# One block for the sum, the norm, the router, the dispatch, the shared expert and q/k/v in a two-layer recurrent and mixture-of-experts kernel

## What is computed

```
xn = layernorm(x)                         # no weights
s  = mamba_like_mixer(xn)                 # layer 0: 64 heads, conv, chunked scan
f  = hadamard_ffn(xn)                     # layer 0: 256 -> 1024 -> 256
x  = x + s * silu(f)
xn = layernorm(x)
s  = causal_attention(xn)                 # layer 1: 16 heads of 16, q/k/v with biases
f  = shared(xn) * sigmoid(xn @ v) + sum of top-4 of 16 experts(xn)   # 704 / 176 hidden
x  = x + s * silu(f)
```

## Time and profile before

| | us |
|---|---|
| profiled execution, its own time | 2469.58 |
| its span | 2467.9 |
| TensorE busy (matmul) | 2181.8, 88% |
| VectorE busy | 1859.4, 75% |
| ScalarE busy | 1146.9, 46% |
| GpSimd busy | 1203.4, 49% |
| granted clock, mean | 0.945 |
| last instruction of the mixer on VectorE | ends 1613.5 |
| shared expert's first gate/up matmul | 1681.8 |
| expert weights asked for, 5632 and 2816 KB | 1790.0, 1790.3 |
| last of the q/k/v weights lands | 1828.2 |
| last value tile of `qkv` | ends 1885.5 |

### The profile page before, as it was taken

The page is one execution under the profiler, slowest core; times in us unless marked ns, Lnnn a source line. Parts: engine busy times, 40 slices in busy tenths (PEclk is TensorE's granted clock), DMA queues, the critical chain, the costliest instruction groups (busy, mean ns, idle before and its releaser), DMA issues. The chain is left out here.

```text
span 2467.9 us, 38890 instructions
## 1 busy us (share of the span) xinstructions
PE 2181.8 (88%) x12914; PEld 1682.4 (68%) x12914; DVE 1859.4 (75%) x3309; ACT 1146.9 (46%) x2397; POOL 1203.4 (49%) x1299
## 2 busy tenths in 40 slices
PE   4995899999999999999999999939946998899982
PEld 2784688888888888888888888728835776344432
DVE  4875788888888888888888888755734444888745
ACT  1331455555555555555555555413323333366660
POOL 3544366565665665656656654603402332999000
PEclk9997799999999999999999999968978999799996
DMA  2002000000000000000000000040053554343214
GB/s 92 1 14 78 30 3 3 33 3 33 3 3 33 3 3 33 3 14 22 3 33 3 3 3 3 3 170 12 1 185 121 179 176 145 107 121 119 78 63 159
DMA packets 76917, 128.87 MB, mean 52 GB/s; under 512 B 22747, under 2 KB 54587, under 8 KB 74715
## 3 DMA queue, kind: packets, MB, share of 16 engines
q1 hardware_dynamic: 69859, 107.64, 13.0%
q0 software_dynamic: 6864, 18.75, 3.1%
HBM read 91.81 MB, written 46.92 MB: 56 GB/s over the span
## 5 line engine op out<-in xcount | busy, mean ns | idle before, releaser
L1026 DVE SCALAR_TENSOR_TENSOR mix_cv<-mix_pp,mix_cw,mix_cv 128x384 f32<-128x384 f32 (+4 forms) x864 | 492.7, 570 | 25.1 <-ACT mix_cv L949 4.2
L873 PEld LDWEIGHTS mix_pyd<-mix_xdt,mix_lm 128*128 128x128 f32 x2048 | 247.8, 192 | 56.7 <-issue 53.1
L949 ACT ACTIVATE mix_cv<-mix_pp,mix_cb,mix_cw 128x384 f32<-128x384 f32 (+1 forms) x288 | 182.1, 632 | 211.2 <-PE mix_pp L80 211.2
L78 PE MATMUL mix_pp<-l0in_XH,mix_wx_lo 128*128 128x384 f32 (+2 forms) x576 | 238.3, 414 | 38.6 <-DVE mix_ss L1015 23.0
L812 POOL TENSOR_TENSOR mix_xdt<-mix_xtok,l_dt 128x512 f32<-128x512 f32 x128 | 133.5, 1043 | 277.9 <-ACT mix_xtok L976 277.9
L805 POOL TENSOR_TENSOR mix_t<-mix_t,mix_xd 128x512 f32<-128x512 f32 x112 | 144.4, 1289 | 219.3 <-DVE mix_t L1040 153.5
L924 PE MATMUL mix_pgt<-mix_wo,mix_gt 128*128 128x256 f32 x1024 | 244.9, 382 | 2.9 <-issue 2.2
L873 PE MATMUL mix_pyd<-mix_xdt,mix_lm 128*128 128x64 f32 x2048 | 243.2, 272 | 2.5 <-DVE mix_lm L1076 2.5
L1839 DVE TENSOR_REDUCE att_tops<-att_psc 128x1 f32<-128x512 f32 (+3 forms) x384 | 189.6, 549 | 48.3 <-PE att_psc L1787 31.5
L955 ACT ACTIVATE mix_pp<-mix_cv 128x384 f32<-128x384 f32 (+1 forms) x288 | 133.0, 462 | 161.6 <-DVE mix_cv L1026 158.8
L924 PEld LDWEIGHTS mix_pgt<-mix_wo,mix_gt 128*128 128x128 f32 x1024 | 184.2, 190 | 31.2 <-issue 9.2
(11 more groups left out here) (365 smaller groups left out, 5794.2 us busy)
## 6 DMA issues: line engine op xcount, KB each, us to landing
mix_w_raw<-in_w_in SPq DMA_DIRECT2D x8, 1280.0 KB, 5.8
y_d<-exp_ys SPq DMA_DIRECT2D x79, 128.0 KB, 1.7
a_part<-att_sums SPq DMA_DIRECT2D x32, 256.0 KB, 5.1
mix_ll<-cs SPq DMA_DIRECT2D x384, 4.0 KB
q<-q SPq DMA_DIRECT2D x12, 512.0 KB, 4.5
k<-k SPq DMA_DIRECT2D x12, 512.0 KB, 4.6
att_qs<-q SPq DMA_DIRECT2D x32, 192.0 KB
att_ks<-k SPq DMA_DIRECT2D x32, 192.0 KB
```

Source lines behind the costliest of these rows:

```text
L78: pe.matmul(out, l_lo, r_hi, start=start, stop=False)
L873: last = pe.matmul(pyd[:, h * HP:(h + 1) * HP], lm[p % 2][:, h, :], xdt[p % 2][:, h * HP:(h + 1) * HP], start=True, stop=True)
L949: act.activation(conv_tile(k), pp[k % 2][:, halo:cols], ACT.Identity, bias=cb[:, it // 2, ct:ct + 1], scale=cw[:, it // 2, ct, 3:4]).then_ ...
L1026: last = dve.scalar_tensor_tensor(out, of, cw[:, g, ct, 3 - d:4 - d], out, ALU.mult, ALU.add)
```

## The change

`combine`, `layernorm`, `shared_and_dispatch` and `qkv` become one block, `middle`. Its parts:

- The silu of layer 0's feed-forward result is taken at the end of `prelude` (tanh on ScalarE, one product on VectorE per block of 512 tokens) before the store.
- Sum, statistics and norm run per block of 512 tokens. Block 0's come first, those of blocks 1 to 3 stand behind units 0 to 5 on VectorE; their power is on GpSimd and their norm on ScalarE (`Identity` with scale and bias) at units 2, 4, 6. Transposes stand in front of units 3 to 8, logits in front of units 0, 5, 7, 9. The weight splits of units 2 to 5 stand behind the low parts of units 0 to 3 on GpSimd.
- The dispatch has 62 steps from unit 9 on, the prefix matmuls are at unit 15, the index matmuls before the third q unit. `opos` and `same` are made with one operation per index (128 operations) from a bfloat16 table; the 16 scaled copies are on ScalarE after units 22 and 23.
- The high and low parts of the units' hidden tile have two buffers instead of three.
- q/k/v weights are loaded at the start and split in units 19 to 21. A q/k unit has its first part and the second on ScalarE, one difference on VectorE, the third part on GpSimd, and one store from a ring of three buffers. Value tiles stand between the q/k units from the fifth on. The factor `DH ** -0.25` on q and k moves into the attention's exponential.
- Gate/up expert weights are asked for after the last sum, down weights on ScalarE's queue at q unit 4.

```diff
+                def gate(b):
+                    rows = X[:, b * 4:(b + 1) * 4, :]
+                    dve.wait_ge(ft_done, b + 1)
+                    dve.scalar_tensor_tensor(rows, ftanh[b], 1.0, rows, ALU.add, ALU.mult).then_inc(f_gated, 1)
...
+                act.wait_ge(cut3, 3)
+                act.wait_ge(turned, 6)
+                for b in range(NB):
+                    act.wait_ge(added, NU - NB + b + 1)
+                    act.activation(ftanh[b], X[:, b * 4:(b + 1) * 4, :], ACT.Tanh, scale=0.5).then_inc(ft_done, 1)
...
+        TURN_AT = {3: 2, 4: 3, 5: 4, 6: 5, 7: 6, 8: 7}
+        NORM_AT = {2: 1, 4: 2, 6: 3}
+        LOGIT_AT = {0: 0, 5: 1, 7: 2, 9: 3}
+        DONE_AT = (0,) * 9 + (3, 9, 15, 21, 27, 32, 39, 42, 48, 50, 52, 54, 56, 57, 60, 60, 60) + (62,) * 14
+        PREFIX_AT, IDX_AT = 15, 2
+        V_AT = 4
...
+                    if b == NB - 1:
+                        sp.dma_start(W[:, 0:WG_COLS], wg_d).then_inc(w_ld, 16)
...
+                    sp.wait_ge(p2_done, u + 1)
+                    sp.dma_start(dst[:, c * P:(c + 1) * P, t * TB:(t + 1) * TB].rearrange("k p t -> p k t"),
+                                 part[u % NR3]).then_inc(stored[u % NR3], 16)
...
+                def power(b):
+                    pool.wait_ge(step, 7 * (b + 1))
+                    pool.tensor_tensor(rstd[:, rows_of(b)], var[:, rows_of(b)], half[:, rows_of(b)], ALU.pow).then_inc(powered, 1)
+                    if b:
+                        pool.wait_ge(powered, 2 * b)
+                        pool.tensor_tensor(shift[:, rows_of(b)], neg[:, rows_of(b)], rstd[:, rows_of(b)], ALU.mult).then_inc(powered, 1)
...
+                power(0)
+                low(0)
+                low(1)
...
+                    if n in (1, 3, 5):
+                        power(n // 2 + 1)
+                    if n < NS - 2:
+                        low(n + 2)
...
+                    pool.wait_ge(p1_done, u + 1)
+                    pool.tensor_tensor(part[u % NR3][:, 2, :], h[u % 2][:, :], part[u % NR3][:, 1, :], ALU.subtract).then_inc(p2_done, 1)
...
+                def turn(p):
+                    pe.wait_ge(xn_ready, p + 1)
+                    wait(pe, lo_done, p if p > 1 else 0)
+                    for j in range(2):
+                        for k in range(KD):
+                            last = pe.transpose(bank_of(p)[:, k * 256 + j * P:k * 256 + (j + 1) * P],
+                                                XN[:, 2 * p + j, k * P:(k + 1) * P], ident[:, :])
+                    last.then_inc(transposed, 1)
...
+                    if n in TURN_AT:
+                        turn(TURN_AT[n])
+                    if n in LOGIT_AT:
+                        logits(LOGIT_AT[n])
...
+                    if u == IDX_AT:
+                        pe.wait_ge(dv, 57)
+                        pe.wait_ge(val_done, 2)
...
+                    if u < 4:
+                        pe.wait_ge(h_done, NU)
+                    else:
+                        pe.wait_ge(sub1, u - 3)
...
+                    if n in NORM_AT:
+                        b = NORM_AT[n]
+                        act.wait_ge(powered, 2 * b + 1)
+                        for t in range(b * 4, b * 4 + 4):
+                            last = act.activation(XN[:, t, :], X[:, t, :], ACT.Identity, bias=shift[:, t:t + 1], scale=rstd[:, t:t + 1])
+                            if t % 2:
+                                last.then_inc(xn_ready, 1)
...
+                    if n in (22, 23):
+                        act.wait_ge(dv, 56)
+                        for t in range((n - 22) * 8, (n - 21) * 8):
+                            last = act.activation(val[:, 4 * t:4 * t + 4, 0, :], same[:, 4 * t:4 * t + 4, :], ACT.Copy, scale=float(t))
+                        last.then_inc(val_done, 1)
...
+                for u in range(len(QK) + 1):
+                    if u < len(QK):
+                        act.wait_ge(mm, u + 1)
+                        wait(act, stored[u % NR3], 16 * (u // NR3))
+                        col = u // 8 * 2 + u // 4 % 2
+                        act.activation(part[u % NR3][:, 0, :], pz[u % 4][:, :], ACT.Identity, bias=bq[:, col:col + 1]).then_inc(p0_done, 1)
+                    if u >= 1:
+                        act.wait_ge(sub1, u)
+                        act.activation(part[(u - 1) % NR3][:, 1, :], h[(u - 1) % 2][:, :], ACT.Copy).then_inc(p1_done, 1)
+                    if u == IDX_AT + 2:
+                        act.wait_ge(split, NS)
+                        act.wait_ge(dv, 62)
+                        act.dma_start(W[0:EI // 2, WG_COLS:], wd_d).then_inc(w_ld, 16)
...
+                        dve.wait_ge(rows_out, 16 * NB)
+                        for i in range((j - 48) * 16, (j - 47) * 16):
+                            last = dve.tensor_scalar(opos[:, i, :], iota[:, :], posf[:, i:i + 1], None, ALU.is_equal)
                     elif j < 56:
-                        at = slice((j - 52) * 16, (j - 51) * 16)
-                        last = dve.tensor_tensor(same[:, at, :], tilef[:, at].unsqueeze(2).to_broadcast([P, 16, TILE_COLS]),
-                                                 table(C_IOTA, TILE_COLS).unsqueeze(1).to_broadcast([P, 16, TILE_COLS]), ALU.is_equal)
+                        for i in range((j - 52) * 16, (j - 51) * 16):
+                            last = dve.tensor_scalar(same[:, i, :], iota[:, 0:TILE_COLS], tilef[:, i:i + 1], None, ALU.is_equal)
...
+                def extra(n):
+                    if n + 1 in TURN_AT:
+                        tokens_lo(TURN_AT[n + 1])
+                    if n in (0, 2, 4):
+                        gate(n // 2 + 1)
+                        residual(n // 2 + 1)
+                    if n in (1, 3, 5):
+                        moments(n // 2 + 1)
...
+                gate(0)
+                residual(0)
+                moments(0)
+                normalise_first()
+                dve.wait_ge(r_hi, 1)
+                dve.tensor_tensor(wrl[:, :, :], wr[:, :, :], wrh[:, :, :].bitcast(F32), ALU.subtract).then_inc(r_lo, 1)
+                tokens_lo(0)
+                tokens_lo(1)
...
+                    dve.scalar_tensor_tensor(h[u % 2][:, :], pz[u % 4][:, :], bq[:, col:col + 1], part[u % NR3][:, 0, :],
+                                             ALU.add, ALU.subtract).then_inc(sub1, 1)
...
+                            act.activation(pr[m % 2][:, AT[k]:AT[k + 1]], pst[k % 2][:, 0:1024 - k * P], ACT.Exp, scale=DH ** -0.5).then_inc(ex_done, 1)
```

More of the change, by code:

```diff
@@ L1164, in shared_and_dispatch @@
-        before = W[0:1, 17408:17408 + SLOTS1 * E].rearrange("p (j e) -> p j e", e=E)
+        stat = s.sb("stat", [P, NT, 6])
+        neg, dif, var, rstd, shift, half = (s.sb(n, [P, NT]) for n in ("neg", "dif", "var", "rstd", "shift", "half"))
+        X0, G0 = (W[:, i * 4096:(i + 1) * 4096].rearrange("p (t d) -> p t d", t=NT) for i in range(2))
+        B = WG_COLS
+        raw = W[:, B:B + 3072].rearrange("p (i b k n) -> p i b k n", i=NS, b=2, k=KD)
+        draw = W[:, B + 3072:B + 4608].rearrange("p (i n) -> p i n", i=NS)
@@ new lines, in middle @@
+        tileu, posu = (W[:, B + 7616 + i * 64:B + 7680 + i * 64].bitcast(U32) for i in range(2))
+        same = W[:, B:B + 2560].bitcast(BF16).rearrange("p (j q) -> p j q", j=NPAIR)
+        val = W[:, B + 2560:B + 7680].bitcast(BF16).rearrange("p (j v q) -> p j v q", j=NPAIR, v=2)
+        before = W[0:1, B:B + SLOTS1 * E].rearrange("p (j e) -> p j e", e=E)
+        XN = VN[:, 0:NT * D].rearrange("p (t d) -> p t d", t=NT)
+        opos = VN[:, 0:NT * D].bitcast(BF16).rearrange("p (j q) -> p j q", j=NPAIR)
@@ L1202, in _, with low @@
+                def low(i):
                     pool.wait_ge(hi_set, i + 1)
@@ new lines, in logits @@
+                def logits(b):
+                    pe.wait_ge(lo_done, 2 * (b + 1))
+                    if b == 0:
+                        pe.wait_ge(r_lo, 1)
+                    for t in range(b * 4, b * 4 + 4):
+                        rows = slice(t * P, (t + 1) * P)
+                        for k in range(KD):
+                            last = matmul3(pe, pr[:, t * NR:(t + 1) * NR], XH[:, k, rows], XL[:, k, rows], wrh[:, k, :], wrl[:, k, :],
+                                           k == 0, k == KD - 1)
+                    last.then_inc(lg_done, 1)
@@ new lines, in normalise_first, with tokens_lo @@
+                def normalise_first():
+                    dve.wait_ge(powered, 1)
+                    for t in range(4):
+                        last = dve.tensor_scalar(XN[:, t, :], X[:, t, :], neg[:, t:t + 1], rstd[:, t:t + 1], ALU.add, ALU.mult)
+                        if t % 2:
+                            last.then_inc(xn_ready, 1)
+                def tokens_lo(p):
+                    dve.wait_ge(hi_done, p + 1)
+                    at = slice(p * 256, (p + 1) * 256)
+                    dve.tensor_tensor(XL[:, :, at], bank_of(p).rearrange("p (k t) -> p k t", k=KD),
```

(1 more changed line is left out.)

544 lines of the change are left out of this document (235 added, 309 removed).

## The result

The changed kernel takes 2452.73 us (median of 4 runs, 2451.03 to 2454.6) against 2473.78 us for the kernel before: 21.05 us less, ratio 0.9914, 95% interval 0.9899 to 0.9928. Forecast were 2421 us and a range of 2397 to 2446. The sign was right and the gain was less than half of the 52 us forecast. The profiled execution took 2453.3 us (span 2451.6), to be set against 2469.6 (span 2467.9).

What follows compares the result with a forecast made beforehand. TensorE was taken as the bound only in the shared-expert units, waiting elsewhere. 20.6 + 147.9 + 50 = 218.5 us against 272.5, with the prelude -51.6, gave 2418.0 profiled and 2421 as median; range 2397 to 2446.

Steps and rivals of the forecast that it cites:

- Before unit 0: From the mixer's end to the first shared-expert unit: unit 0 starts 20.6 us after the mixer instead of 68.5.
- stops: Early shared-expert units: TensorE waits before units 2 to 5 and 7 for weight splits and norms, 13.0 us in sum.
- lock and clock: Shared-expert units: 3 us for VectorE and GpSimd excluding each other, 3 us for clock falls after one and a half stops.
- Rival 2: Units and q/k/v: TensorE bound throughout, stops and clock counted twice; units 15 and q/k/v 7 less, 2399 us; chance 0.22.
- Rival 3: Shared-expert units: the clock stays at 1.2 GHz, making the kernel slower, 2490 to 2510 us; chance 0.04.
- Comparisons: Units 18 to 21: 128 one-index comparisons at 0.1 us each, 3.3 a unit, costing 1.5 us in all, up to 12.
- Scaled copies on ScalarE, the last output: After units 22 and 23: sixteen scaled copies move from VectorE to ScalarE, delaying the last output, +1.8 us.
- Down-weight load: q/k/v: 2.8 MB asked for on ScalarE's queue in q unit 4, taking 13 us with over 30 us left.
- rival 1: q/k/v and units: stop moves to stores and queues, q/k/v 65 us, 2445 in all; chance 0.22 shared with another rival.
- q/k/v without the load: q/k/v: two units share the ring's wait and a store's landing, giving 2.8 us a unit and 50 us in all.
- Lock in units 18 to 21: Units 18 to 21: short comparisons let GpSimd's low parts return to 1.29 us; about 3 us either way with the splits.
- Prelude: End of the prelude: a tanh and a product stand behind the last addition, +2.4 us.

Runs made afterwards that it cites:

- experiment 11: Large comparisons and down-weight load in 12 pieces, plus GpSimd's first low part waiting for the first four normalisations, against the changed kernel: 2432.94 us, ratio 0.9835 to before.
- experiment 10: Changed kernel with a down-weight load of 512 columns and each 16 comparisons as one instruction, indices set to 0 (part of the computation left out): 2418.27 us.
- experiment 6: As experiment 5, but both operands of the 8 large comparisons in bf16: 2431.54 us, ratio 0.9841 to the kernel before.
- experiment 3: Changed kernel with only 512 of 8192 columns of the down-weight load, leaving out 15 of 16 experts' down weights: 2434.11 us, ratio 0.9851 to before.
- experiment 7: Changed kernel with small comparisons spread over eight units, multiples, index product and v later, load pieces in q/k/v units 8 to 15: 2440.62 us.
- experiment 8: As experiment 7, with the large comparisons in the same places: 2431.64 us, ratio 0.9844 to the kernel before.
- experiment 4: Changed kernel with the 128 small comparisons put back to the 8 large ones of the kernel before: 2445.44 us, ratio 0.99 to before.
- experiment 5: Changed kernel with the down-weight load in 12 pieces and the large comparisons together: 2427.88 us, ratio 0.9837 to the kernel before.
- experiment 2: Changed kernel with the down-weight load at the same place as 16 transfers with rows of 2 KB: 2443.43 us, ratio 0.9884 to before.
- experiment 9: As experiment 5, with comparisons moved less far than in experiment 8, index product at q/k/v unit 4, v and load pieces from unit 5: 2432.72 us.

## Why the prediction was wrong, step by step

Two steps failed: the price of the small comparisons, and the down-weight load, whose effect on the stores was put at nothing in the forecast.

- **Before unit 0** (20.6 forecast): 22.1, of which 1.3 is the meeting of normalisations and low part (experiment 11). I had priced the normalisations by the row of before, where GpSimd was idle. (The terms of this step add up to 1633.8, not 1634.1.)
- **Units 0 to 9, with norms, turns and early stops**: held in the total, and not in its terms. From VectorE's product of unit 0 to that of unit 9 it takes 69.2 us; nine units of the base (4.66 each), 3.3 of transposes, 7.7 of logits, 13.0 of stops (their terms add up to 12.9) and 6 of lock and clock make 72.0. The stops are where the walk put them: in front of units 2 (4.54 idle, 3.4 forecast), 4 (1.26, 2.2 forecast for units 3 and 4), 5 (2.79, 4.2 forecast) and 7 (2.60, 3.1 forecast), 11.2 in all. The clock cost more than the 3 us taken: it is at 0.50 from 1653 to 1659, 1677 to 1683 and 1694 to 1700, after each of the three long stops and not after one and a half of them. With TensorE busy in nearly all of these 18 us that is some 9 us, an estimate. So the other terms were too high by some 9 us together, the stops by 1.8 of them. Rival 2 had named one way for that, stops and clock counted twice; it was not separated further, and that the total came out so near is in part luck. Rival 3 is refuted: 1.00 from 1704 to 1762.6.
- **Units 9 to 18**: 44.3, forecast 44.7 with the prefix's 2.7.
- **Comparisons**: the first failed step. "0.1 taken, 0.05 and 0.25 the ends: 3.3 a unit, 1.5 us in all, up to 12 at the far end". They take 0.20 to 0.24 (over 0.2 was the prediction's own sign of being wrong), and 13 to 16 us in time. The nearest row has 320 columns in 0.363; I scaled it by the columns to 0.1. A row with one size cannot tell the fixed part from the rate, and the fixed part is nearly all: 0.21 of 0.25 us (experiment 10). The far end was wrong as a sum too: at 0.25 each a unit has 32 x 0.25 + 1.4 = 9.4 us on VectorE against 4.2 on TensorE, which is 20.8 us in four units and not 12. The comparisons are 28.3 us of VectorE work in four units, where the large ones of before were 17.0. The Trainium skill (VectorE: DVE Perf Modes, "The TRN2 errata — SBUF-src ops pay a fixed extra latency per instruction") states a measured fixed part of about 150 cycles and advises operands of 512 elements or more. By its figures 128 columns at four a cycle take (150 + 32) / 0.96 GHz = 0.19 us, an estimate; the trace agrees in kind and has 0.246. On the same page ("What auto-detection actually checks") the Trainium skill says that the engine takes the 16-bit mode open to two-input operations only if every tensor is 16-bit with a step of one. In experiment 6 the positions are repeated along the columns, so their step is not one, and the trace agrees (2766 ns against 2767, no change).
- **Scaled copies on ScalarE, the last output**: 1.8 forecast. Not tested alone. From unit 18 to unit 23 it takes 38.8 us; 5 x 4.66, the comparisons' 1.5 and this 1.8 make 26.6. With the comparisons nearly gone (experiment 10) it is 25.2, so these terms were right together, and the 12.2 missing are the comparisons'.
- **Down-weight load** ("13 us, and there are over 30 us left"): the second failed step. I asked whether the load would be in time for its reader and not whom it would hold up while it ran. The stop was in rival 1, but as 6 us landings over five units with three causes at once (-28 us, 2445); it came as one wait of 20.6 us and 18 to 19 us in time. Nearer than the forecast in time, then, and not right in its mechanism: it was the length of the load's rows, and neither the ring's depth alone (experiment 3) nor landings of 6 us in general. The Trainium skill (DMA: Bandwidth & Descriptors, "Queues, rings and completion order") says that each DMA engine takes turns between queues packet by packet. By that a queue whose packets are long gets most of the time, which fits the trace: 34 packets against 33 between 1830 and 1838, 29 KB against 1 KB, and the shorter wait with 2 KB rows (20.6 to 4.9 us). The packet of that section is a group of several descriptors; in this trace the turns are of one row each, and the measurement decides.
- **q/k/v without the load**: 2.8 a unit forecast, 2.55 found in experiment 3.
- **Lock in units 18 to 21**: GpSimd's low parts take 1.29 to 1.32 us beside the small comparisons and 1.8 to 2.6 beside the large ones, as the rule quoted in the prediction has it. VectorE was the bound there, so this gain brought no time.
- **Prelude**: +2.4 forecast, the mixer's first load comes 1.8 later. At the mixer's last add it is 2.0 to 3.7 in seven of the twelve profiled executions with the new prelude, and 5.0 to 5.5 in five, the kernel after (5.2) among them; see the last section.
- **Sum**: with both failed terms removed the kernel takes 2418.3 us, 2.7 from the forecast. They make 34.5 us of time, 31.1 from last add to gather, and the miss was 31.7. The stretch itself is less exact than the time: 223.4 us in experiment 10 against 219.5 by the forecast (273.5 - 54.0). The forecast also added 3.3 us from the profiled execution to the median, which the changed kernel does not show (2453.3 and 2452.7); such differences cancel in part.

## What to carry to other kernels

Price a small instruction from two rows of different size, or from the smallest row there is, and work out the far end of the range with the same sum as the middle. If 80 and 128 columns would cost the same, splitting one large instruction into sixteen is a loss as soon as its engine is near the bound. For a large transfer ask two questions: when is it needed, and who else moves data while it runs; a load in pieces of 0.24 MB between small stores gave back 13 of 18 us without any other change. And look at what lies behind before moving work: in experiments 7 and 8 what the units gained was lost again in q/k/v.

## What the runs showed of the hardware

- The small comparisons spare GpSimd, the large ones do not. Low parts (L1190) of the kernel after, then of experiment 4:

```profile
1770.12 1.29 POOL L1190 TENSOR_TENSOR mid_hl<-mid_h,mid_hh 128x512 fp32r<-128x512 f32 x1 [6.46 <-ACT mid_hh L1347]
```

```profile
1766.59 2.58 POOL L1190 TENSOR_TENSOR mid_hl<-mid_h,mid_hh 128x512 fp32r<-128x512 f32 x1 [4.21 <-ACT mid_hh L1347]
```

- A tensor-by-scalar comparison in bf16 takes 0.235 us for 80 and 0.246 for 128 columns (medians, kernel after), 0.55 for 1280 and 0.75 for 2048 (experiment 10; the means there are 0.64 and 1.03, with those that meet a GpSimd operation). The tensor-by-tensor form with broadcast operands takes 1.97 and 2.77 in the mean for the last two and 2.28 at the shortest for 2048, in fp32 and in bf16 alike (experiments 5 and 6).
- A load whose rows are 32 KB holds stores of 1 KB rows on another queue back for 20 us; in rows of 2 KB ScalarE's waits for such stores stay under 5. Fifteen issues in a row on ScalarE take 0.49 us each (experiment 2).
- The clock can fall in the mixer's last product. TensorE in the kernel after and in experiment 5:

```profile
1610.00:1612.00 2.00, 0.57 (x2) 0.93 0.00 0
1612.00:1614.00 2.00, 2.00 (x6) 0.50 0.00 0
1614.00:1616.00 2.00, 1.51 (x7) 0.71 0.00 0
```

```profile
1612.00:1614.00 2.00, 1.31 (x9) 1.00 0.00 0
```

The five executions with 0.50 from 1612 to 1614 (the kernel after, experiments 2, 7, 8 and 9) reach the mixer's last add 5.0 to 5.5 us later than the kernel before, the seven without it 2.0 to 3.7. The timed runs of one kernel lie apart by as much (2426.8 to 2427.9 and 2432.4 to 2433.4 in experiment 5); that this is the same cause was not shown.
